# One visit of TensorE's column tiles for both value products of a full pair of key blocks, with the sums' PSUM bank lent to the scores

## The chip, the core and the metric

The program runs on one core of one Trainium2 chip. The metric is the device time of one execution in microseconds (us). TensorE multiplies matrices and writes PSUM, which has eight banks of 128 x 512 numbers of 32 bits; VectorE (DVE) and ScalarE (ACT) read PSUM; GpSimd (POOL) works in SBUF; SyncE (SP) and POOL issue DMAs. Semaphores are all that orders the engines against each other, and each engine runs its own list of instructions in order.

## The reference

Input x is 2 x 2048 x 512. A layer norm is followed by causal attention with 16 heads of 32 features (rotary positions on queries and keys), a residual, a second layer norm, and a linear layer with a routed low-rank part (8 experts, top 2) and a residual. The part that matters here:

```
scores = einsum('bhqd,bhkd->bhqk', q, k) / sqrt(32), later keys masked
attn = softmax(scores)              # needs each query's maximum and sum
ctx = einsum('bhqk,bhkd->bhqd', attn, v)
```

## The kernel before, in words

Three stages follow one another: `project` (queries, keys, values into scratch tensors in HBM), `attend`, and `finish`. The change touches `attend` alone.

**Groups, units, steps and pairs.** `attend` runs over 8 groups of 4 heads (`HG = 4`, `GROUPS = 8`). In a group the 2048 queries are 4 units of 512 (`QT`), and unit t meets its keys in blocks of 128: 4(t+1) steps, 40 in all (`STEPS`, `NSTEP`, L57). Two steps are a pair (`NPAIR = 20`). The last pairs of the units are 1, 5, 11 and 19 (`LAST_PAIR`). The last two pairs of each unit lie on the causal diagonal. The other 12 of a group are full: pairs 2, 3; 6 to 9; 12 to 17. `GATHER[p]` (L75) is set for exactly these, and says where their probabilities are added up for the sums.

**Scores.** Of each step four matmuls (`scores`, L970 to L983), one for each head, 98 x 128 by 98 x 512 in the full array, write 128 keys by 512 queries each into one of three PSUM banks of `a_st` in turn. ACT takes the exponential of each into the SBUF ring `a_probs` (L1077), which holds 4 steps; ACT fills a pair's places once the pair two before it has been used by the value product and added up (L1065 to L1071). A score waits until ACT is done with the bank (`wait_score_bank`, L786).

**Values.** `values` (L985 to L1000) multiplies a step's probabilities by the values of its 128 keys, for four heads at once: TensorE works there as four column tiles of 128 x 32 (`tile_position=(0, h * DK)`). The operands are of 32 bits, and each product is two matmul instructions in the trace, so that a step shows 8. All steps of a unit add up in one bank, `a_av`; ACT copies it out at the unit's end (L1062).

**Sums.** POOL adds the two steps of a pair (L936), in full pairs into the two buffers of `a_gather`, the later ones by way of `a_pair` and a DMA that accumulates (L833). `sums` (L1002 to L1026) multiplies by ones, also in column tiles, into the bank `a_sum`. It runs in the two diagonal pairs of a unit alone. At the start of the next unit's first pair (the opening pair: 2, 6, 12, or 0 of the next group) DVE transposes the bank (L1095, `turn_sums`, which raises `sum_turned`), inverts it (L1099) and turns it back (L1104). These three stand on DVE ahead of the first item of that pair, behind the first and behind the second.

**Items.** The softmax needs each query's maximum before its scores are taken. These maxima are found ahead of use by items: 140 in a group (`ITEMS`, `NITEM`), each one product of 96 x 128 by 96 x 512 (or less) in the full array into one of three banks of `a_mx` in turn (`item`, L957; `item_products`, L227), and one maximum on DVE (`item_max`, L241: a reduction at L249, or an addition of the mask and a maximum at L252). An item waits for the maximum of the one three before it (L967). A planner (`plan_items`, L107) spreads them over the pairs: 6 or 7 in most pairs, 8 in pairs 7 and 14, 6 in the opening pairs 2, 6 and 12. In the last group there are none from pair 10 on (`NO_ITEMS`); there the scores use six banks (three of `a_st`, three of `a_mx`), and DVE adds the pairs. In the first group the pairs 0 to 3 have 15 items each.

**TensorE's order** is written out in `group` (L1028 to L1043). Iteration p issues the scores of pair p+1 and the values of pair p, in two halves. A half takes half of the items, each followed by one of a step's four scores, and then one visit of the column tiles for one value product:

```python
for half, due in enumerate((items[:middle], items[middle:])):
    s = 2 * p + 2 + half
    for i in range(max(HG, len(due))):
        if i < len(due):
            item(...)
        if i < HG and s < NSTEP:
            scores(g, par, s, i)
    values(g, par, 2 * p + half)
sums(g, p)
```

PSUM is full: three banks of scores, three of items, one of values, one of sums.

Of the kernel before, what the change touches and what calls it, by code (L numbers as in the profile page):

```python
# [41 lines left out]
HG = 4  # L42
GROUPS = BATCH * HEADS // HG
QT = SEQ // TT
# [7 lines left out]
START = 1  # L52
# [4 lines left out]
STEPS = [(t, j) for t in range(QT) for j in range((t + 1) * SUB)]  # L57
NSTEP = len(STEPS)
# [4 lines left out]
LAST_PAIR = [e // 2 for e in UNIT_END]  # L63
# [11 lines left out]
GATHER = [gather_of(p) for p in range(NPAIR)]  # L75
# [46 lines left out]
def items_before(p, first):  # L122

    steady = PLAN[p % NPAIR] + NITEM * (p // NPAIR)
    return min(BEFORE_FIRST + PER_FIRST * p, steady) if first else steady
# [5 lines left out]


NO_ITEMS = min(p for p in range(NPAIR) if items_before(p, False) >= NITEM)


def units_ended_at_pair(p, first):
# [589 lines left out]
def attend(nc, block, qk_scr, v_scr, ctx_scr, shared, first, early):  # L726
    with ExitStack() as ctx:
# [6 lines left out]
        BANKS, MX_BANKS = 3, 3  # L734
# [14 lines left out]
        st_ps = ctx.enter_context(nc.psum_tensor("a_st", [P, BANKS, TT], F32))  # L749
        mx_ps = [ctx.enter_context(nc.psum_tensor(f"a_mx{n}", [P, TT], F32)) for n in range(MX_BANKS)]  # L750
        av_ps = ctx.enter_context(nc.psum_tensor("a_av", [P, TT], F32))
        sum_ps = ctx.enter_context(nc.psum_tensor("a_sum", [P, TT], F32))
# [8 lines left out]
        av_copied, sum_turned = early.av_copied, early.sum_turned  # L761
# [11 lines left out]
        def uses_before(n, of, banks):  # L773

            return n - banks if n >= banks else max(m for m in range(of) if m % banks == n) - of

        SIX_FROM = HG * (2 * NO_ITEMS + 2)

        def score_bank(g, n):

            if g < GROUPS - 1 or n < SIX_FROM:
                return st_ps[:, n % BANKS]
            m = (n - SIX_FROM) % (2 * BANKS)
            return st_ps[:, (SIX_FROM + m) % BANKS] if m < BANKS else mx_ps[m - BANKS][:, :]

        def wait_score_bank(pe, g, n):  # L786

            if g < GROUPS - 1 or n < SIX_FROM + BANKS:
                pe.wait_ge(exp_done, HG * NSTEP * g + uses_before(n, HG * NSTEP, BANKS) + 1 + BANKS)
            elif n < SIX_FROM + 2 * BANKS:  # L790
                pe.wait_ge(max_done, NITEM * GROUPS + MX_BANKS)
            else:
                pe.wait_ge(exp_done, HG * NSTEP * g + n - 2 * BANKS + 1 + BANKS)
# [162 lines left out]
        def _(pe):  # L956
# [13 lines left out]
            def scores(g, par, s, h):  # L970

                t, j = STEPS[s]
                q0 = max(0, j - t * SUB) * P
                if (g, h, t, j) == (0, 0, 0, 0):
                    pe.wait_ge(key_ones, 1)
                if (g, h, t, j) == (0, 0, 2, 2 * SUB):
                    pe.wait_ge(ones_copied, 4 * 16)
                if j == 0 and h == 0:
                    pe.wait_ge(shift_loaded[t % 2], SHIFTS * (2 * g + t // 2 + 1) + START)
                n = HG * s + h  # L980
                wait_score_bank(pe, g, n)
                block = keys[par][j // SUB][0:98, h, j % SUB * P:(j % SUB + 1) * P]
                pe.matmul(score_bank(g, n)[:, q0:TT], block, queries[t][0:98, h, q0:TT], start=True, stop=True).then_inc(st_done, 1)  # L983

            def values(g, par, s):  # L985

                t, j = STEPS[s]
                q0 = max(0, j - t * SUB) * P
                if j >= t * SUB:
                    pe.wait_ge(masked, diagonal_steps(g, s))  # L990
                else:
                    pe.wait_ge(exp_done, exps(g, s, HG - 1))
                if j == 0:
                    pe.wait_ge(av_copied, 4 * g + t + START)
                for h in range(HG):
                    mm = pe.matmul(av_ps[h * DK:(h + 1) * DK, q0:TT], vb[par][:, j, h * DK:(h + 1) * DK],  # L996
                                   probs[:, s % RING, h, q0:TT], start=j == 0, stop=s in UNIT_END,
                                   tile_position=(0, h * DK))
                if s % 2:
                    mm.then_inc(values_done, 1)  # L1000

            def sums(g, p):  # L1002

                s = 2 * p
                t, j = STEPS[s]
                if GATHER[p]:
                    return
                unit_first, unit_last = p == LAST_PAIR[t] - 1, p in LAST_PAIR
                q0, q1 = (max(0, j + n - t * SUB) * P for n in range(2))
                if unit_first:  # L1010
                    pe.wait_ge(sum_turned, 4 * g + t + START)
                if p in GATHERED_SUMS:
                    a = GATHERED_SUMS[p]
                    pe.wait_ge(gather_joined[a], 16 * joined(NPAIR * g + p, a))
                    for h in range(HG):
                        pe.matmul(sum_ps[h * DK:(h + 1) * DK, :], ones[:, :], gather[:, a, h, :], start=unit_first, stop=False,  # L1016
                                  tile_position=(0, h * DK))
                if q1 > q0:
                    for h in range(HG):
                        pe.matmul(sum_ps[h * DK:(h + 1) * DK, q0:q1], ones[:, :], probs[:, s % RING, h, q0:q1],  # L1020
                                  start=unit_first and p not in GATHERED_SUMS, stop=False, tile_position=(0, h * DK))
                pe.wait_ge(pair_added, 2 * (NPAIR * g + p) + 2)
                for h in range(HG):
                    mm = pe.matmul(sum_ps[h * DK:(h + 1) * DK, q1:TT], ones[:, :], pair[:, p % 2, h, q1:TT],  # L1024
                                   start=False, stop=unit_last, tile_position=(0, h * DK))
                mm.then_inc(pair_done, 1)  # L1026

            def group(g, par, use, next_use, first, last):  # L1028
                for p in range(NPAIR):
                    items = [(n, k) for n, k in items_of_pair(p, first) if not (n and last)]  # L1030
                    middle = (len(items) + 1) // 2
                    for half, due in enumerate((items[:middle], items[middle:])):
                        s = 2 * p + 2 + half
                        for i in range(max(HG, len(due))):
                            if i < len(due):
                                n, k = due[i]
                                item(g + n, (par + n) % 2, next_use if n else use, k)
                            if i < HG and s < NSTEP:
                                scores(g, par, s, i)
                            elif i < HG and not last:  # L1040
                                scores(g + 1, 1 - par, s - NSTEP, i)
                        values(g, par, 2 * p + half)
                    sums(g, p)  # L1043

            pe.wait_ge(first.mul_done, 4 * TILES + PROJECT_AHEAD)
# [662 lines left out]
```

## Time and profile before

| | |
|---|---|
| median of 3 runs | 1568.57 us (1568.54 to 1571.94) |
| the profiled execution | 1570.34 us |
| its span, first to last instruction | 1568.6 us |
| TensorE busy, mean granted clock | 98%, 0.998 |
| DVE, ACT, POOL busy | 73%, 49%, 57% |
| `attend` in the span | about 310 to 1296 us |
| one group of heads in the steady part | about 122.8 us (742.00 to 864.85, the same DVE instruction in two groups) |

A view of the chain of work follows what ended last back through what released it; its pieces show how long TensorE really spent on each group of matmuls. In the timeline a matmul's duration is modelled and overlaps the next one, so the distance from one start to the next is the figure to read. "PEld" is the loading of weights.

### The profile page before, as it was taken

How to read it: one execution, taken by the hardware profiler on the slowest of the kernel's cores; microseconds unless marked ns; L12 is line 12 of the kernel's file. 1: busy time of each engine (PE TensorE's matmuls, PEld its weight loads, DVE VectorE, ACT ScalarE, POOL GpSimd, SP SyncE). 2: the span in 40 equal slices, each digit the busy share in tenths (PEclk: the TensorE clock that was granted, in tenths of full speed). 3: DMA queues.
4: the chain of work that ended last, by engine and by line, in shares of the span. 5: the costliest groups of instructions: out<-in, count | busy, mean ns of one | idle time of the engine just before them, and what ended most of it. 6: DMA issues, size and time to landing. Idle time of an engine off the chain costs nothing.

```text
span 1568.6 us, 24836 instructions
## 1 busy us (share of the span) xinstructions
PE 1537.8 (98%) x9088; PEld 966.5 (62%) x9088; DVE 1141.6 (73%) x2269; ACT 767.6 (49%) x1540; POOL 890.7 (57%) x597
## 2 busy tenths in 40 slices
PE   6999999999999999999999999999999989999999
PEld 5888887755555555555555555555555537777777
DVE  6766666797777777777777777777777777656665
ACT  3222222236666656656666666665666673223221
POOL 2232322547778778787788797787787821121111
PEclk9999999999999999999999999999999999999999
DMA  5555685793485376377368359358444364222321
GB/s 201 208 198 191 214 270 193 201 195 70 86 173 127 85 166 143 82 150 167 83 135 189 82 123 201 81 107 197 96 92 122 85 145 132 81 81 86 143 67 54
DMA packets 120403, 215.83 MB, mean 138 GB/s; under 512 B 12504, under 2 KB 45784, under 8 KB 113112
## 3 DMA queue, kind: packets, MB, share of 16 engines
q1 hardware_dynamic: 102384, 136.20, 32.1%
q0 software_dynamic: 8064, 58.72, 18.2%
q10 hardware_dynamic: 9840, 19.40, 3.5%
q8 instruction: 69, 1.13, 0.3%
q14 instruction: 46, 0.38, 0.1%
HBM read 96.23 MB, written 58.72 MB: 99 GB/s over the span
## 4 chain that ended last, share of the span: by engine, by line
PE 90%; DVE 5%; DMA 2%; ACT 1%; issue 1%; SPq 0%; POOL 0%; DVEq 0%; POOLq 0%; ACTq 0%
PE a_mx L234 20%; PE a_av L996 16%; PE a_st L983 15%; PE p_pair L492 10%; PE f_wo_ps L1333 6%; PE f_out_ps L1393 5%; PE p_v L504 5%; PE a_sum L1016 2%; DVE a_part L249 2%; PE a_sum L1024 2%; PE f_out_ps L1408 1%; PE f_mid_ps L1333 1%; PE f_lg_ps L1363 1%; PE a_mx L238 1%; DMA a_gather<-a_pair 1%
## 5 line engine op out<-in xcount | busy, mean ns | idle before, releaser
L1077 ACT ACTIVATE a_probs<-a_st 128x512 f32<-128x512 f32 (+2 forms) x1244 | 584.6, 536 | 363.6 <-PE a_st L983 358.4
L249 DVE TENSOR_REDUCE a_part<-a_mx 128x1 f32<-128x512 f32 (+2 forms) x842 | 537.5, 680 | 104.3 <-PE a_mx L234 88.6
L936 POOL TENSOR_TENSOR a_pair<-a_probs 128x1024 f32<-128x1024 f32 (+2 forms) x224 | 397.8, 1800 | 39.4 <-ACT a_probs L1077 16.2
L936 POOL TENSOR_TENSOR a_gather<-a_probs 128x1024 f32<-128x1024 f32 x76 | 179.6, 2384 | 99.1 <-ACT a_probs L1077 99.1
L252 DVE CUSTOM_DVE_ANT_0 a_mx<-a_mx,f_ctx 128x384 f32<-128x384 f32 (+1 forms) x240 | 148.7, 632 | 86.8 <-PE a_mx L234 86.7
L366 POOL TENSOR_TENSOR p_rot<-p_mul 128x1024 f32<-128x1024 f32 x32 | 87.5, 2734 | 194.1 <-DVE p_mul L670 194.1
L1326 POOL TENSOR_TENSOR f_x<-f_x,f_bias 128x512 f32<-128x512 f32 x32 | 40.2, 1286 | 204.9 <-DVE f_xn L1543 204.9
L996 PE MATMUL a_av<-a_probs,a_v 128*32 128x512 f32 (+3 forms) x1280 | 149.8, 540 | 1.3 <-POOL a_probs L917 1.3
L996 PE MATMUL a_av<-a_probs,shared 128*32 128x512 f32 (+3 forms) x1280 | 150.9, 543 | 0.0
L917 POOL TENSOR_SCALAR_AFFINE_SELECT a_probs<-a_probs 128x512 f32<-128x512 f32 x128 | 89.8, 733 | 60.9 <-ACT a_probs L1077 60.7
L234 PE MATMUL a_mx<-a_k_stack,a_q_stack 96*128 96x512 f32 (+3 forms) x320 | 119.3, 397 | 0.0
L234 PEld LDWEIGHTS a_mx<-a_k_stack,a_q_stack 96*128 96x128 f32 x320 | 58.7, 189 | 71.6 <-DVE a_part L249 59.1
L983 PE MATMUL a_st<-a_q_stack,a_k_stack 98*128 98x512 f32 (+3 forms) x287 | 99.1, 366 | 1.4 <-DMA a_q_stack<-a_neg_rows 1.4
L578 ACT ACTIVATE p_rot_hi<-p_rot 128x1024 fp32r<-128x1024 f32 x32 | 34.0, 1061 | 110.1 <-POOL p_rot L366 94.3
L234 PE MATMUL a_mx<-a_k_stack,a_third 96*128 96x512 f32 (+3 forms) x192 | 73.6, 410 | 0.4
L674 DVE TENSOR_TENSOR p_rot_lo<-p_rot,p_rot_hi 128x1024 fp32r<-128x1024 f32 x28 | 45.8, 1635 | 36.6 <-ACT p_rot_hi L578 36.6
L492 PE MATMUL p_pair<-p_xt_lo,p_w_hi 128*128 128x512 f32 x256 | 69.9, 394 | 0.0
L833 POOL DMA_DIRECT2D a_gather<-a_pair x56 | 49.2, 879 | 33.9 <-POOL a_pair L936 15.1
L669 DVE TENSOR_TENSOR p_mul<-p_pair,p_tab 128x1024 f32<-128x1024 f32 x32 | 39.0, 1220 | 39.8 <-PE p_pair L492 39.8
L234 PE MATMUL a_mx<-a_k_stack,a_q_first 96*128 96x512 f32 (+3 forms) x192 | 65.3, 378 | 1.8 <-DVE a_part L249 1.1
L983 PE MATMUL a_st<-a_third,a_k_stack 98*128 98x512 f32 (+3 forms) x189 | 67.1, 375 | 0.0
L983 PEld LDWEIGHTS a_st<-a_q_stack,a_k_stack 98*128 98x128 f32 x287 | 53.9, 190 | 17.3 <-ACT a_probs L1077 8.2
(218 smaller groups left out, 2829.0 us busy)
## 6 DMA issues: line engine op xcount, KB each, us to landing
a_gather<-a_pair POOLq DMA_DIRECT2D x56, 1024.0 KB, 7.0
qk_scratch<-p_rot_hi SPq DMA_DIRECT2D x32, 512.0 KB, 3.1
qk_scratch<-p_rot_lo SPq DMA_DIRECT2D x32, 512.0 KB, 3.9
a_k_stack<-qk_scratch SPq DMA_DIRECT2D x60, 256.0 KB, 8.1
a_q_first<-qk_scratch SPq DMA_DIRECT2D x48, 256.0 KB, 6.6
a_third<-qk_scratch SPq DMA_DIRECT2D x36, 256.0 KB, 5.5
v_scratch<-p_v_st SPq DMA_DIRECT2D x32, 256.0 KB, 7.1
ctx_scratch<-a_ctx_st SPq DMA_DIRECT2D x32, 256.0 KB, 2.8
```

Of the source, the lines that this page charges most:

```text
L234: mm = pe.matmul(places[:, i, :], queries[0:96, head, qi * P:(qi + 1) * P], keys[0:96, head, 0:width], start=(i == 0), stop=not masked_her ...
L249: dve.tensor_reduce(found, scores.rearrange("p (h n) -> p h n", n=width), AX.X, ALU.max).then_inc(self.max_done, 1)
L252: dve.tensor_tensor_reduce(out=scores, in0=scores, in1=self.mask[:, TT - width:TT], scale=1.0, scalar=3.0 * MASKED, op0=ALU.add, op1=ALU.m ...
L366: pool.tensor_tensor(rot[:, par], mul[:, par, :, 0, :], mul[:, par, :, 1, :], ALU.add).then_inc(rot_done, 1)
L492: mm = pe.matmul(pair_ps[p % 2][:, half, :], w[:, kt, cols], a[u][:, kt, :], start=(n == 0), stop=(n == len(passes) - 1))
L504: mm = pe.matmul(v_ps[s % 2][:, :], a[u][:, kt, s * P:(s + 1) * P], w[:, kt, 2 * DM:3 * DM], start=(n == 0), stop=(n == len(passes) - 1))
L917: pool.affine_select(block, block, pattern=[[0, HG], [1, P]], compare_op=ALU.is_ge, fill=0.0, base=0, channel_multiplier=-1).then_inc(mask ...
L936: pool.tensor_tensor(place[:, h:h + 2, q0:TT], probs[:, s % RING, h:h + 2, q0:TT], probs[:, (s + 1) % RING, h:h + 2, q0:TT], ALU.add).then ...
L983: pe.matmul(score_bank(g, n)[:, q0:TT], block, queries[t][0:98, h, q0:TT], start=True, stop=True).then_inc(st_done, 1)
L996: mm = pe.matmul(av_ps[h * DK:(h + 1) * DK, q0:TT], vb[par][:, j, h * DK:(h + 1) * DK], probs[:, s % RING, h, q0:TT], start=j == 0, stop=s ...
L1077: act.activation(probs[:, s % RING, h, q0:TT], score_bank(g, HG * s + h)[:, q0:TT], ACT.Exp, scale=SCORE_SCALE).then_inc(exp_done, 1)
L1333: mm = pe.matmul(out, w, a, start=(n == 0), stop=(n == len(pairs) - 1))
```

## The change

In iterations with a full pair (`GATHER[p]`) the two halves become one: all items of the pair, interleaved with all eight scores of the two steps ahead, then both value products in one visit of the column tiles. In the other iterations the two halves stay.

The eight scores in a row get a fourth bank: the bank of the sums, which is idle while full pairs are worked on. A plan (`plan_banks`) gives each score of the two-half and one-visit iterations its bank, the one used longest ago, with the fourth allowed in full iterations only and, in an opening iteration, from the third score on. The first score in it there waits for the transposition of the sums (`sum_turned`); the first sums of a unit wait for the exponential of the last score that lay in their bank.

```diff
+def plan_banks():
+    banks, behind, ahead_of_sums, last_use = {}, {}, {}, [None] * SCORE_BANKS
+    for n in range(-2 * HG, GROUPS * SCORES - 2 * HG):
+        g, p, i = n // SCORES, n % SCORES // (2 * HG), n % (2 * HG)
+        score = n + 2 * HG
+        if score >= SCORES * (GROUPS - 1) + SIX_FROM:
+            break
+        opens = n >= 0 and p - 1 in LAST_PAIR
+        if n >= 0 and GATHER[p] and opens and i == 0:
+            last_use = last_use[:SCORE_BANKS] + [-(QT * g + STEPS[2 * p][0])]
+        usable = range(SCORE_BANKS + 1 if n >= 0 and GATHER[p] and not (opens and i < 2) else SCORE_BANKS)
+        bank = min(usable, key=lambda b: -1 if last_use[b] is None else max(0, last_use[b]))
+        banks[score], behind[score], last_use[bank] = bank, last_use[bank], score
+        if bank == SUM_BANK:
+            ahead_of_sums[QT * g + STEPS[2 * p][0]] = score
...
         def score_bank(g, n):
             if g < GROUPS - 1 or n < SIX_FROM:
-                return st_ps[:, n % BANKS]
+                bank = BANK_OF_SCORE[SCORES * g + n]
+                return sum_ps[:, :] if bank == SUM_BANK else st_ps[:, bank]
...
         def wait_score_bank(pe, g, n):
-            if g < GROUPS - 1 or n < SIX_FROM + BANKS:
-                pe.wait_ge(exp_done, HG * NSTEP * g + uses_before(n, HG * NSTEP, BANKS) + 1 + BANKS)
+            if g < GROUPS - 1 or n < SIX_FROM:
+                behind = BANK_BEHIND[SCORES * g + n]
+                if behind is not None and behind < 0:
+                    pe.wait_ge(sum_turned, -behind + START)
+                elif behind is not None:
+                    pe.wait_ge(exp_done, behind + 1 + BANKS)
...
                 if unit_first:
                     pe.wait_ge(sum_turned, 4 * g + t + START)
+                    if QT * g + t in AHEAD_OF_SUMS:
+                        pe.wait_ge(exp_done, AHEAD_OF_SUMS[QT * g + t] + 1 + BANKS)
...
                     middle = (len(items) + 1) // 2
-                    for half, due in enumerate((items[:middle], items[middle:])):
-                        s = 2 * p + 2 + half
-                        for i in range(max(HG, len(due))):
+                    visits = [(items, (0, 1))] if GATHER[p] else [(items[:middle], (0,)), (items[middle:], (1,))]
+                    for due, steps in visits:
+                        ahead = [(2 * p + 2 + half, h) for half in steps for h in range(HG)]
+                        for i in range(max(len(ahead), len(due))):
...
-                        values(g, par, 2 * p + half)
+                        for half in steps:
+                            values(g, par, 2 * p + half)
```

The banks of the items stay three, and their order and number in each pair stay as they are. No engine's instructions change in number or shape.

## Rows read from the trace of the kernel before

**Rows 1.** The page: busy time of the engines, and the chain's shares by engine.

```profile
PE 1537.8 (98%) x9088; PEld 966.5 (62%) x9088; DVE 1141.6 (73%) x2269; ACT 767.6 (49%) x1540; POOL 890.7 (57%) x597
...
PE 90%; DVE 5%; DMA 2%; ACT 1%; issue 1%; SPq 0%; POOL 0%; DVEq 0%; POOLq 0%; ACTq 0%
```

**Rows 2.** One stretch of steady attention: busy us and instructions of PE, PEld, DVE, ACT, POOL.

```profile
820.00:940.00 120.00, 119.45 (x809) 64.34 (x812) 93.32 (x201) 75.92 (x162) 96.94 (x66) 1.00 0.59 129
```

**Rows 3.** The chain, 700 to 760 us: start, us, engine, tile, line.

```profile
710.80 0.36 PE a_av L996 x8
...
734.38 0.86 PE a_sum L1016 x8
...
737.59 0.99 PE a_av L996 x8
```

**Rows 4.** Timeline of full pairs 7 and 8, 736 to 757 us: start, us, engine.

```profile
742.16 2.06 ACT L1077 ACTIVATE a_probs<-a_st 128x512 f32<-128x512 f32 x4 [0.81 <-PE a_st L983]
...
743.05 0.39 PE L983 MATMUL a_st<-a_third,a_k_stack 98*128 98x512 f32 x1
743.38 1.06 PE L996 MATMUL a_av<-a_probs,a_v 128*32 128x512 f32 x8
744.37 0.44 PE L234 MATMUL a_mx<-a_k_stack,a_q_stack 96*128 96x384 f32 x1
...
747.38 0.50 PE L234 MATMUL a_mx<-a_k_stack,a_q_stack 96*128 96x512 f32 x1
747.72 0.40 PE L983 MATMUL a_st<-a_third,a_k_stack 98*128 98x512 f32 x1
747.96 0.40 PE L234 MATMUL a_mx<-a_k_stack,a_q_stack 96*128 96x512 f32 x1
```

**Rows 5.** Timeline, 400 to 445 us: first item of a half, and DVE's maxima.

```profile
436.76 0.50 PE L234 MATMUL a_mx<-a_k_stack,a_third 96*128 96x512 f32 x1
...
437.30 2.48 DVE L249 TENSOR_REDUCE a_part<-a_mx 128x1 f32<-128x512 f32 x4 [1.08 <-PE a_mx L234]
```

**Rows 6.** Timeline of opening pair 6, a steady group: TensorE's first item, then DVE.

```profile
735.61 0.50 PE L234 MATMUL a_mx<-a_k_stack,a_q_stack 96*128 96x512 f32 x1
...
735.75 0.72 DVE L1095 STREAM_TRANSPOSE a_sum_t<-a_sum 128x512 f32<-128x512 f32 x1 [1.34 <-PE a_sum L1024]
...
736.39 0.65 DVE L249 TENSOR_REDUCE a_part<-a_mx 128x1 f32<-128x512 f32 x1
...
738.28 0.53 DVE L252 CUSTOM_DVE_ANT_0 a_mx<-a_mx,f_ctx 128x384 f32<-128x384 f32 x1
```

**Rows 7.** Opening pair 2 of the first group, eight items in its first half: timeline.

```profile
332.74 0.45 PE L234 MATMUL a_mx<-a_third 96*128 96x384 f32 x1
...
335.46 0.65 DVE L249 TENSOR_REDUCE a_part<-a_mx 128x1 f32<-128x512 f32 x1
...
336.17 0.50 PE L234 MATMUL a_mx<-a_k_first,a_third 96*128 96x512 f32 x1 [0.69 <-DVE a_part L249]
```

**Rows 8.** Pair 1 of the first group, second half, eight items: timeline.

```profile
323.88 0.50 PE L234 MATMUL a_mx<-a_k_first,a_third 96*128 96x512 f32 x1
...
324.42 3.68 DVE L249 TENSOR_REDUCE a_part<-a_mx 128x1 f32<-128x512 f32 x6 [0.88 <-PE a_mx L234]
...
327.55 0.51 PE L234 MATMUL a_mx<-a_k_first,a_third 96*128 96x512 f32 x1 [0.16 <-DVE a_part L249]
```

**Rows 9.** Waits, 400 to 1250 us: waiter, releaser, us in total, times, longest.

```profile
ACT a_probs L1077 <- PE a_st L983: 312.0, 325, 3.0
...
DVE a_sum_t L1095 <- PE a_sum L1024: 17.5, 20, 1.3
...
PE a_mx L234 <- DVE a_part L249: 1.9, 7, 0.3
```

**Rows 10.** The last group without items, timeline: first visits of two iterations in a row.

```profile
1262.07 1.07 PE L996 MATMUL a_av<-a_probs,a_v 128*32 128x512 f32 x8
...
1266.31 1.06 PE L996 MATMUL a_av<-a_probs,a_v 128*32 128x512 f32 x8
```

More of the change, by code:

```diff
@@ L133 @@
 NO_ITEMS = min(p for p in range(NPAIR) if items_before(p, False) >= NITEM)
+SCORES = HG * NSTEP
+SIX_FROM = HG * (2 * NO_ITEMS + 2)
+SCORE_BANKS = 3
+SUM_BANK = SCORE_BANKS
+def plan_banks():
[13 more added lines that the diff above has]
+            ahead_of_sums[QT * g + STEPS[2 * p][0]] = score
+    return banks, behind, ahead_of_sums, sorted(range(SCORE_BANKS), key=lambda b: last_use[b]), last_use
+BANK_OF_SCORE, BANK_BEHIND, AHEAD_OF_SUMS, OLDEST_FIRST, LAST_USE = plan_banks()
 def units_ended_at_pair(p, first):
@@ L775, in uses_before @@
             return n - banks if n >= banks else max(m for m in range(of) if m % banks == n) - of
-        SIX_FROM = HG * (2 * NO_ITEMS + 2)
         def score_bank(g, n):
             if g < GROUPS - 1 or n < SIX_FROM:
-                return st_ps[:, n % BANKS]
+                bank = BANK_OF_SCORE[SCORES * g + n]
+                return sum_ps[:, :] if bank == SUM_BANK else st_ps[:, bank]
             m = (n - SIX_FROM) % (2 * BANKS)
-            return st_ps[:, (SIX_FROM + m) % BANKS] if m < BANKS else mx_ps[m - BANKS][:, :]
+            return st_ps[:, OLDEST_FIRST[m]] if m < BANKS else mx_ps[m - BANKS][:, :]
         def wait_score_bank(pe, g, n):
-            if g < GROUPS - 1 or n < SIX_FROM + BANKS:
-                pe.wait_ge(exp_done, HG * NSTEP * g + uses_before(n, HG * NSTEP, BANKS) + 1 + BANKS)
+            if g < GROUPS - 1 or n < SIX_FROM:
[4 more added lines that the diff above has]
+                    pe.wait_ge(exp_done, behind + 1 + BANKS)
+            elif n < SIX_FROM + BANKS:
+                pe.wait_ge(exp_done, LAST_USE[OLDEST_FIRST[n - SIX_FROM]] + 1 + BANKS)
             elif n < SIX_FROM + 2 * BANKS:
@@ L1037, in group @@
                                 item(g + n, (par + n) % 2, next_use if n else use, k)
[L1038 to L1041, printed above, removed]
-                        values(g, par, 2 * p + half)
+                            if i < len(ahead):
+                                s, h = ahead[i]
+                                if s < NSTEP:
+                                    scores(g, par, s, h)
+                                elif not last:
+                                    scores(g + 1, 1 - par, s - NSTEP, h)
+                        for half in steps:
+                            values(g, par, 2 * p + half)
                     sums(g, p)
```

## The prediction

> **What bounds the kernel now.** I read the page first. TensorE is busy for 98% of the span and is 90% of the chain that ended last; DVE is 5% [rows 1]. A busy matmul row only says that one was in flight, so the next view is the stretch of steady attention: in 120 us TensorE is busy 119.45 us, DVE 93.32, ACT 75.92, POOL 96.94 [rows 2]. The waits say the same from the other side: ACT waits for TensorE's scores 312 us in 850, DVE waits for the sums 20 times (some 28 units end in that stretch), and TensorE itself is held by DVE for 1.9 us [rows 9]. So TensorE's own time sets the pace, and DVE has some 22% to spare on average. Whether it has it at the right moment is the question of this case.
>
> The last view, the timeline of full pairs, shows what a visit of the column tiles costs beyond its work. Read starts, not durations. Full-array matmuls follow each other every 0.235 us (0.24 from the first score to the next item) [rows 4]. (a) From the last score to the visit it is 0.33 us: 0.10 too much. (b) The visit takes 0.99 us for 512 queries and 0.36 for 128, hence 0.21 per 128 queries and 0.84 to 0.86 for the work itself; a product that follows inside the same visit takes 0.86 [rows 3], so 0.13 is entry. (c) The first item after it takes 0.34 us to the next start [rows 4], 0.10 too much, since its weights were not loaded ahead. Together 0.33 us a visit.
>
> **What the change takes away.** One visit in each full pair: 12 pairs in 8 groups, 96 visits. 96 x 0.33 = 31.7 us, all on TensorE and so on the path, if nothing takes its place. The Trainium skill ("TensorEngine Tiling (Array Packing)", Key Properties) says that changing the tiling mode drains the engine, which is the same gap told as a mechanism; by that rule alone the time would fall by those 31.7 us.
>
> **What it adds: items in one burst.** Number and order of the items stay, but all of a pair now stand ahead of one long visit of 0.99 + 0.86 = 1.85 us, where each half with its 3 or 4 items had a visit behind it in which DVE caught up. An item waits for the maximum of the one three before. The prices: DVE starts 0.54 us after the first item starts (436.76 to 437.30), takes 0.60 us an item (four take 2.48, six take 3.68, the last ends 0.68 after its start) [rows 5, 8], and a waiting item starts 0.06 us after the maximum it waits for (335.46 + 0.65, then 336.17) [rows 7]. Its successor is then 0.10 us later too, as in (c). Items in a burst would start at 0, 0.575, and every 0.47 from there, since a score stands between.
>
> *Regular full pairs* (3; 7 to 9; 13 to 17). Item k is needed at 0.575 + 0.47(k-1) and can start at 0.54 + 0.60(k-3) + 0.68 + 0.06. For the sixth item (k = 5) that is 2.45 against 2.48; for the seventh 2.92 against 3.08, with the 0.10 a delay of 0.26; for the eighth 3.39 against 3.68, a delay of 0.39. The present kernel has such a burst, eight items in a half of the first group's pair 1: the eighth starts at 327.55, 0.06 behind its maximum (324.42 + 4 x 0.60 + 0.68 = 327.50) [rows 8]. So a pair of seven gains 0.33 - 0.26 = 0.07 us and a pair of eight loses 0.06. A group has seven of the first and two of the second: 0.37 us gained, 2.7 us over the groups (the last has four such pairs with items).
>
> The same page's Performance Considerations ("PSUM Bottleneck") speak against the change: tiling speeds up TensorE but not the emptying of PSUM, which may become the bottleneck. The trace agrees for a burst (0.60 us an item against 0.47) and not for the average [rows 2]. By that rule alone regular pairs would gain nothing and the sum would be 2.7 us higher.
>
> *Opening pairs* (2, 6, 12). DVE transposes the sums ahead of the first maximum and turns the inverse back behind the second. In pair 6 TensorE's first item starts at 735.61, and DVE reaches the first maximum at 736.39 and the third at 738.28, 2.67 us behind [rows 6]. Now half a pair, three items, ends there and no item waits. In the burst the sixth item needs the third maximum: 2.67 + 0.65 + 0.06 = 3.38 us, where it could have started at 2.45. The wait is 0.93, with the successor's 0.10 it is 1.03 us; less 0.33 the pair is 0.70 us slower. The first group's pair 2 shows the very wait: the sixth item of its half of eight starts 3.43 us after the first, and the wait named is for DVE [rows 7]. Three in each of seven groups and two in the last (12 has no items there): 23 x 0.70 = 16.1 us. No later wait gives this back, as TensorE has almost none [rows 9].
>
> **The other edits.** *The fourth bank of scores:* ACT needs 2.06/4 = 0.515 us a score [rows 4] against TensorE's 0.47; with three banks the last of eight would wait some 0.1 to 0.2 us, with four none: nought here. *The wait for `sum_turned`* in front of the third score: that score is due 0.34 + 0.94 = 1.28 us behind the first item, the transposition ends 0.14 + 0.72 = 0.86 behind it [rows 6], with a release of 0.06 and 0.10 for weights 1.02: covered by 0.26 us. If DVE were later by one maximum (0.60), 0.35 us would show. Queued behind this wait are all items and values of the pair. *The wait of the first sums* for an exponential two iterations old: covered by a whole iteration, nought. *Values one visit later:* `values_done` rises at an iteration's end as now, and ACT, which fills the ring behind it, idles waiting for TensorE [rows 9]; POOL's additions (96.94 of 120) move up to 1.2 us within the iteration and have a whole one until ACT asks; no DMA is moved past another. Nought.
>
> **The tail of the last group.** Pairs 12 to 17 have no items. An iteration takes 4.24 us (1262.07 to 1266.31) [rows 10]. New, TensorE needs 8 x 0.235 + 0.33 + 1.71 = 3.9 us and ACT 8 x 0.515 = 4.12 [rows 4]: ACT bounds, 0.12 x 6 = 0.7 us gained; nothing, if the joining DMAs bound there, and 2.0 at most.
>
> **Sum.** -2.7 + 16.1 - 0.7 = +12.7 us. The profiled execution took 1570.34 us (span 1568.6, 1.7 around it), 1.8 above the median of 1568.57; counted from the median: 1581 us. What a measurement of this kernel can tell from no change is about 0.3%, 4.7 us.
>
> **Bounds.** The opening pairs' net can lie between -0.33 (no wait) and +1.1 (DVE late by another 0.4); I take 0.70 for the two rows that show it. The regular pairs' lies between -0.17 (each maximum 0.1 us less late, since masked items of 384 columns are shorter) and +0.1. That makes 1562 to 1594 without a change of mechanism.
>
> **Rivals.**
> 1. *DVE keeps up: faster.* Its 22% of idle time [rows 2] speaks for it; the bursts of rows 7 and 8 speak against. It decides at the items' wait: if the seventh item of a regular pair and the sixth of an opening one start without one, 90 pairs gain 0.33 and the tail 0.7: 1538 us. 12%. Where only the openings' wait is a third of what I say (0.3 us), it is 23 x 0 - 6 (the regular pairs at -0.09) - 0.7: 1562 us, 6%.
> 2. *No difference that can be told.* The opening pairs cost 0.2 to 0.3 us each, as DVE's transposition moves ahead or the long visit hides part: 23 x 0.25 - 3.4 = +2.4: 1571 us. 14%.
> 3. *The lent bank costs as well.* DVE is not idle when the sums end in some 8 cases of 28 [rows 9], and the third score waits 0.35 us in every opening: +8 us, 1589; if it also pushes the items, up to 1600. 12%.
> 4. *The change does not save the visit.* The second product pays its own 0.33: +43 us, 1611. The 0.86 behind a value product [rows 3] excludes it nearly: 2%.
>
> My own forecast, 1581, has 54%. Left out of a range of 1557 to 1595 are rival 1's full form, rival 4 and the end of rival 3, some 17%. Faster 0.18, same 0.14, slower 0.68.
>
> **What the profile of the changed kernel would show.** Two value products as one piece of about 1.85 us, and no first-item gap between them. In opening pairs the sixth item about 3.4 us behind the first, its wait put down to DVE; in regular pairs the seventh at about 3.1. TensorE's waits for DVE in 400 to 1250 us up from 1.9 to 20 us or more, DVE idle mostly during the long visits. A group of heads at about 124.5 us (122.8 + 3 x 0.70 - 0.37). I am wrong if the group is at or below 122.8, or if the waits at the items are there and the group is not longer: then TensorE had slack that I did not see.

## The result, and the profile after

The changed kernel takes 1581.09 us (median of 9 runs) against 1570.0 us for the kernel before on the same chip: ratio 1.0071, 95% interval 1.005 to 1.0093, or 8 to 15 us slower. The forecast was 1581 us, 12.7 us above the median of before. One of the nine executions of the kernel before took 5023.35 us; the median hardly depends on it. Executions of one kernel spread by some 11 us with the mean granted clock (the kernel before in another series: 1567.48 us at 1.000, 1579.02 us at 0.991), so that two medians that lie less than about 3 us apart are not told apart here.

The page of the changed kernel, its busy times and the chain's shares by engine, beside [rows 1]:

```profile
PE 1539.3 (97%) x9088; PEld 966.1 (61%) x9088; DVE 1133.5 (72%) x2269; ACT 767.4 (49%) x1540; POOL 890.3 (56%) x597
...
PE 86%; DVE 10%; DMA 1%; issue 1%; ACT 1%; SPq 0%; POOL 0%; DVEq 0%; POOLq 0%; ACTq 0%
```

The instructions are the same in number. DVE did no more work than before, yet its share of the chain went from 5% to 10%: TensorE now stands behind it. The same stretch of steady attention as [rows 2] (busy us of PE, PEld, DVE, ACT, POOL):

```profile
820.00:940.00 120.00, 117.88 (x801) 63.35 (x799) 90.44 (x197) 75.43 (x160) 93.23 (x64) 1.00 0.56 125
```

TensorE has lost 1.6 us of its 119.45, and every other engine did less in the 120 us: the whole pipeline runs slower. The waits of TensorE for DVE in 400 to 1250 us (in total, times, longest): first the line of the kernel before that [rows 9] leaves out, beside its 1.9 us behind L249, then the two of the changed kernel:

```profile
PE a_mx L234 <- DVE a_part L252: 1.0, 6, 0.2
...
PE a_mx L262 <- DVE a_part L277: 9.1, 20, 0.6
PE a_mx L262 <- DVE a_part L280: 3.7, 13, 0.4
```

Together 2.9 us before and 12.8 us now. These lines understate the waits, since a matmul's modelled duration covers part of one: the sixth item below is given 0.38 us of waiting, but it starts 0.78 us behind the score before it (742.64), where 0.235 is usual. So the distances between starts are read here. Opening pair 6 of a steady group, which answers to [rows 6], in the timeline:

```profile
740.11 0.50 PE L262 MATMUL a_mx<-a_k_stack,a_q_stack 96*128 96x512 f32 x1
...
740.25 0.72 DVE L1134 STREAM_TRANSPOSE a_sum_t<-a_sum 128x512 f32<-128x512 f32 x1 [1.34 <-PE a_sum L1059]
...
740.88 0.65 DVE L277 TENSOR_REDUCE a_part<-a_mx 128x1 f32<-128x512 f32 x1
...
742.16 0.69 DVE L1143 STREAM_TRANSPOSE a_rsum_b<-a_rsum 128x512 f32<-128x512 f32 x1
...
742.78 0.53 DVE L280 CUSTOM_DVE_ANT_0 a_mx<-a_mx,f_ctx 128x384 f32<-128x384 f32 x1
...
743.42 0.50 PE L262 MATMUL a_mx<-a_k_stack,a_q_stack 96*128 96x512 f32 x1 [0.38 <-DVE a_part L280]
...
744.56 1.93 PE L1029 MATMUL a_av<-a_probs,a_v 128*32 128x512 f32 x16
...
746.42 0.44 PE L262 MATMUL a_mx<-a_k_stack,a_q_stack 96*128 96x384 f32 x1
```

DVE reaches the third maximum (742.78) 2.67 us behind the pair's first item, to the hundredth as before, and the sixth item (743.42) stands right behind it, 3.31 us after the first. The visit is one piece of 16 instructions. The iteration takes 6.31 us (740.11 to 746.42); before it took 5.76, from 735.61 [rows 6] to 741.37. Three more lines of that iteration of the kernel before: its last two scores of the first half, the visit, and the next pair's first item:

```profile
736.82 0.76 PE L983 MATMUL a_st<-a_third,a_k_stack 98*128 98x512 f32 x2
...
737.52 1.06 PE L996 MATMUL a_av<-a_probs,a_v 128*32 128x512 f32 x8
...
741.37 0.44 PE L234 MATMUL a_mx<-a_k_stack,a_q_stack 96*128 96x384 f32 x1
```

From the first of the two scores to the visit it is 0.70 us, where 0.235 + 0.33 would do: the kernel before already lost 0.13 us in this pair, to a score that waited until ACT was done with its bank. In the changed kernel the chain runs over DVE at the sixth item (start, us, engine, tile, line):

```profile
742.16 0.69 DVE a_rsum_b L1143
742.85 0.46 DVE a_mx L280
743.42 0.50 PE a_mx L262
...
744.63 1.85 PE a_av L1029 x16
```

Opening pair 2 of the next group suffers more. Its two ends in the timeline:

```profile
839.73 0.50 PE L262 MATMUL a_mx<-a_third,a_q_stack 96*128 96x512 f32 x1
...
846.44 0.50 PE L262 MATMUL a_mx<-a_third,a_q_stack 96*128 96x512 f32 x1
```

6.71 us against 5.78: DVE first has the five short operations that end a unit's maxima, and reaches the transposition of the sums 0.52 us behind the first item (840.25), in pair 6 only 0.14. Pair 12 takes 6.37 against 5.90. The three openings of a group together are 1.95 us longer, 0.65 each.

A regular pair of eight items, pair 7 (its first item, its eighth, its visit, the next pair's first item):

```profile
746.42 0.44 PE L262 MATMUL a_mx<-a_k_stack,a_q_stack 96*128 96x384 f32 x1
...
750.05 0.45 PE L262 MATMUL a_mx<-a_k_stack,a_q_stack 96*128 96x512 f32 x1
...
750.65 1.92 PE L1029 MATMUL a_av<-a_probs,a_v 128*32 128x512 f32 x16
...
752.51 0.50 PE L262 MATMUL a_mx<-a_k_stack,a_q_stack 96*128 96x512 f32 x1
```

The eighth item comes 3.63 us behind the first, the pair takes 6.09 us against 6.01 [rows 4]: what the spared visit gave went to the waits. A whole group, from one masked maximum of pair 7 to the same one a group later (747.05 to 871.45), takes 124.40 us against 122.85: 1.55 more. Less the 1.95 of the openings, the nine regular pairs are 0.40 us faster together. For the changed kernel that is the longest of six groups: over the second to the seventh group the mean is 124.11 us against 122.73, or 1.38 more. By the medians of these six, the regular pairs are far from equal: 3, 13, 15, 16 and 17 gain 0.10 to 0.22 us, pair 8 gains 0.02, 7 and 14 lose 0.06 and 0.10, and pair 9 loses 0.23. In pair 9 the seventh item, the first of the next group, stands behind scores of 384 columns, and its wait for DVE grew from 0.29 to 0.61 us (before, after):

```profile
757.82 0.64 PE L234 MATMUL a_mx<-a_k_first,a_q_first 96*128 96x128 f32 x4 [0.29 <-DVE a_part L249]
...
762.30 0.64 PE L262 MATMUL a_mx<-a_k_first,a_q_first 96*128 96x128 f32 x4 [0.61 <-DVE a_part L277]
```

The tail of the last group, first visits of two iterations in a row, beside [rows 10]:

```profile
1272.71 1.92 PE L1029 MATMUL a_av<-a_probs,a_v 128*32 128x512 f32 x16
1276.76 1.92 PE L1029 MATMUL a_av<-a_probs,a_v 128*32 128x512 f32 x16
```

4.05 us where it was 4.24; over the five distances from 1272.71 to the sixth visit at 1293.14 the mean is 4.09. Nothing of it reaches the end of the stage. From the start of pair 12's iteration in the last group to the last transposition of the sums it is 35.46 us before and 36.62 us after. In pair 18 the first value product waits for POOL, which masks the probabilities of the diagonal; the wait was 1.29 us in the kernel before:

```profile
1297.99 1.94 PE L1029 MATMUL a_av<-a_probs,a_v 128*32 128x512 f32 x8 [2.26 <-POOL a_probs L950]
```

### The profile page after: what moved, and what is told of

Its sections match the earlier page's. It is cut to its first block, busy times and chain, and to the rows that moved or that the text cites. A ratio compares the mean times of both kernels' runs of the same rounds, so it can differ in the third digit from the quotient of the medians.

```text
span 1579.4 us, 24843 instructions
## 1 busy us (share of the span) xinstructions
PE 1539.3 (97%) x9088; PEld 966.1 (61%) x9088; DVE 1133.5 (72%) x2269; ACT 767.4 (49%) x1540; POOL 890.3 (56%) x597
## 4 chain that ended last, share of the span: by engine, by line
PE 86%; DVE 10%; DMA 1%; issue 1%; ACT 1%; SPq 0%; POOL 0%; DVEq 0%; POOLq 0%; ACTq 0%
PE a_mx L262 18%; PE a_av L1029 16%; PE a_st L1016 11%; PE p_pair L520 10%; PE f_wo_ps L1372 6%; PE f_out_ps L1432 5%; PE p_v L532 5%; DVE a_part L277 5%; PE a_sum L1016 2%; PE a_sum L1051 2%; PE a_sum L1059 2%; PE f_out_ps L1447 1%; PE f_mid_ps L1372 1%; PE f_lg_ps L1402 1%; DVE a_rsum_b L1143 1%
## 5 line engine op out<-in xcount | busy, mean ns | idle before, releaser
L1116 ACT ACTIVATE a_probs<-a_st 128x512 f32<-128x512 f32 (+1 forms) x1064 | 512.5, 531 | 363.8 <-PE a_st L1016 337.5
L1029 PE MATMUL a_av<-a_probs,a_v 128*32 128x512 f32 (+3 forms) x1280 | 141.4, 542 | 2.3 <-POOL a_probs L950 2.3
L1029 PE MATMUL a_av<-a_probs,shared 128*32 128x512 f32 (+3 forms) x1280 | 141.8, 543 | 0.0
L262 PE MATMUL a_mx<-a_k_stack,a_q_stack 96*128 96x512 f32 (+3 forms) x320 | 123.4, 409 | 3.8 <-DVE a_part L277 1.8
L1116 ACT ACTIVATE a_probs<-a_sum 128x512 f32<-128x512 f32 (+1 forms) x180 | 105.7, 587 | 10.8 <-PE a_sum L1016 8.6
L1016 PE MATMUL a_st<-a_q_stack,a_k_stack 98*128 98x512 f32 (+3 forms) x243 | 84.8, 360 | 0.8 <-DMA a_q_stack<-a_neg_rows 0.8
L1029 PEld LDWEIGHTS a_av<-a_probs,a_v 128*32 128x32 f32 x1280 | 30.4, 109 | 61.0 <-issue 39.1
```

The source lines that it names most:

```text
L262: mm = pe.matmul(places[:, i, :], queries[0:96, head, qi * P:(qi + 1) * P], keys[0:96, head, 0:width], start=(i == 0), stop=not masked_her ...
L1116: act.activation(probs[:, s % RING, h, q0:TT], score_bank(g, HG * s + h)[:, q0:TT], ACT.Exp, scale=SCORE_SCALE).then_inc(exp_done, 1)
```

## The experiments

Theory: the items of a full pair, 6 to 8 in one burst, wait for their three banks, that is for DVE, above all in the opening pairs, where DVE's two transpositions stand among the maxima. Rivals: each merged visit costs a little; the lent bank and its wait for the transposition cost. Ratios are against the kernel before on the same chip. What the traces say of the opening pairs and of a whole group stands in a table behind the experiments.

**Openings put back into two halves.**

```diff
-visits = [(items, (0, 1))] if GATHER[p] else [...]
+visits = [(items, (0, 1))] if GATHER[p] and not p - 1 in LAST_PAIR else [...]
```

> The changed kernel with the opening pairs (2, 6, 12) put back into two halves; the nine other full pairs keep one visit. My theory (the loss sits in the opening pairs, where DVE's two transpositions stand ahead of the maxima that the burst of items needs): the 11 us are gone, the time is 0 to 4 us below the kernel before, about 1568 us, and a group of heads takes 122.5 us. Rival (each merged visit costs a little, since DVE falls behind in every burst): three quarters of the merged pairs are left, so 8 us of the 11 stay, about 1578 us. Rival (the lent bank costs): the bank is still lent in the openings, so 1581 us stays.

1570.34 us, ratio 0.9986 (0.9966 to 1.0006): level with the kernel before (1570.14 us in this series), where 0 to 4 us below it were expected; a group takes 122.25 us in the trace, where 122.5 were. The loss is gone with three of twelve merged pairs, while nine stay merged. The rival that each merged visit costs a little falls.

**The opposite: one visit in the openings alone.**

```diff
-visits = [(items, (0, 1))] if GATHER[p] else [...]
+visits = [(items, (0, 1))] if GATHER[p] and p - 1 in LAST_PAIR else [...]
```

> The opposite of e1: one visit in the opening pairs alone, two halves in the nine other full pairs. My theory: all of the loss stays, 1580 to 1585 us. Rival (every burst costs a little): a quarter of the 11 us, about 1573 us.

1583.33 us, ratio 1.007 (1.0044 to 1.0096): the whole loss, from a quarter of the merged pairs.

**DVE turns the inverse back last.**

```diff
-                        for unit in ended:
-                            if i == 0:
-                                invert(*unit)
-                            if i == 1:
-                                turn_back(*unit)
...
+                    for unit in ended:
+                        invert(*unit)
+                        turn_back(*unit)
```

> The changed kernel with DVE's inversion and its turning back of the sums moved behind all items of the opening pair; the first transposition stays where it is. My theory: the third maximum of an opening pair then ends at about 0.78 + 1.2 + 0.65 = 2.6 us instead of 3.3 us behind the first item, the sixth item waits 0.1 to 0.2 us instead of 0.9, and the kernel returns to within 3 us of the one before: 1568 to 1573 us. Rival (the third score waits for the transposition of the sums in the lent bank): that transposition has not moved, so 1581 us stays. Rival (POOL's division waits for the turned inverse and holds its additions): slower than 1581 us.

1567.75 us, ratio 0.9971 (0.9954 to 0.9988), some 13 us below the changed kernel and just under the range expected. The rival of POOL's division, which wanted a slower kernel, falls too. The same opening pair in its timeline (first item, first two maxima, third maximum, sixth item, next pair's first item):

```profile
730.99 0.50 PE L262 MATMUL a_mx<-a_k_stack,a_q_stack 96*128 96x512 f32 x1
...
731.76 1.25 DVE L277 TENSOR_REDUCE a_part<-a_mx 128x1 f32<-128x512 f32 x2
...
732.94 0.56 DVE L280 CUSTOM_DVE_ANT_0 a_mx<-a_mx,f_ctx 128x384 f32<-128x384 f32 x1
...
733.63 0.46 PE L262 MATMUL a_mx<-a_k_stack,a_q_stack 96*128 96x512 f32 x1
...
736.58 0.45 PE L262 MATMUL a_mx<-a_k_stack,a_q_stack 96*128 96x384 f32 x1
```

The third maximum starts 1.95 us behind the first item instead of 2.67, the sixth item 2.64 instead of 3.31, and the iteration takes 5.59 us instead of 6.31. The transposition of the sums, for which the lent bank waits, did not move (0.13 us behind the first item, 0.14 in the changed kernel), so the lent bank is not the cause. The move took 0.70 us off each of the three openings. It did more than undo the loss: a group takes 122.03 us against 122.73 in the kernel before, so with the burst's wait shortened the merged visits begin to pay.

**The same order in the kernel before**, as a control (the edit is the one above, the rest is the kernel before):

> The kernel before (two halves everywhere) with DVE's inversion and turning back moved behind the opening pair's items, as in e2. It tells whether e2's gain of 13 us against the changed kernel is the removal of the burst's wait or a gain that this order gives anyway. My theory: in two halves no item waits for the turning back, so nothing moves: 1570 us, within 2 us. Rival (the order gains by itself): 1557 to 1562 us.

1570.23 us, ratio 0.9998 (0.998 to 1.0016). The order gains nothing where items come in halves; in e2 it took away a wait that the burst had made.

**Three banks for the scores.**

```diff
-usable = range(SCORE_BANKS + 1 if n >= 0 and GATHER[p] and not (opens and i < 2) else SCORE_BANKS)
+usable = range(SCORE_BANKS)
```

> The changed kernel with one visit, but the scores keep three banks and the sums' bank is never lent. My theory: ACT's 0.515 us a score against TensorE's 0.47 us costs 0.1 us at the end of a burst at most, and often nothing where an item waits anyway: 0 to 6 us above the changed kernel, 1581 to 1587 us. Rival (the lent bank's wait for the transposition is what costs): 8 us below the changed kernel, about 1573 us.

1583.17 us, ratio 1.0066 (1.0039 to 1.0092). Without the lent bank the change costs the same, and the opening pairs take the same time to 0.01 us (6.70, 6.29 and 6.37): the bank neither hurts nor helps where the items wait anyway.

**The lent bank alone, two halves everywhere.**

```diff
-visits = [(items, (0, 1))] if GATHER[p] else [(items[:middle], (0,)), (items[middle:], (1,))]
+visits = [(items[:middle], (0,)), (items[middle:], (1,))]
```

> The changed kernel with two halves and two visits everywhere, and the lent fourth bank for the scores alone. My theory: the scores hardly wait for a bank, so 0 to 2 us below the kernel before, 1569 us. Rival (the lent bank's wait for the transposition costs): 1575 us or more.

1569.34 us, ratio 0.9993 (0.9973 to 1.0014): nothing that can be told. In the trace pair 6 takes 5.60 us instead of 5.76: the score that waited for its bank in the kernel before waits no longer.

**One visit, and the bank goes to the items.** Starting from the kernel before, with the merged visits of the change:

```diff
+def plan_item_banks():
...
+                usable = range(MAX_BANKS + 1 if GATHER[p] and not (opens and i < 3) else MAX_BANKS)
+                bank = min(usable, key=lambda b: -1 if last_use[b] is None else max(0, last_use[b]))
...
-                pe.wait_ge(max_done, NITEM * g + uses_before(k, NITEM, MX_BANKS) + 1 + MX_BANKS)
-                first.item_products(pe, mx_ps[k % MX_BANKS], k, queries[t], keys[par][c])
+                behind = ITEM_BEHIND[NITEM * g + k]
+                if behind is not None and behind < 0:
+                    pe.wait_ge(sum_turned, -behind + START)
+                elif behind is not None:
+                    pe.wait_ge(max_done, behind + 1 + MX_BANKS)
+                first.item_products(pe, item_bank(g, k), k, queries[t], keys[par][c])
```

> The merged visit of the change, but the sums' bank is lent to the items as a fourth bank in full pairs (from the fourth item on in an opening pair) and the scores keep three banks. My theory (items, not scores, lack a bank): an item then waits for the maximum of the one four before, 0.60 us later slack, so the seventh and eighth items of a regular pair no longer wait, and the sixth of an opening pair waits for the second maximum instead of the third; the 0.33 us of each merged visit stays as gain in most pairs: 17 to 22 us below the kernel before, about 1551 us. Rival (DVE as a whole cannot keep the pace, whatever the banks): 1575 us or more.

1548.34 us, ratio 0.9852 (0.983 to 0.9874), 22.4 us below the kernel before of its series (17 to 22 were expected). So the spared visits are worth having once the items have a bank more: same DVE, same order on it, same number of maxima. "DVE as a whole cannot keep the pace" falls. The profiled execution took 1558.18 us, 10 us above the median; the lines are from a stretch at a granted clock of 1.00. Its opening pair (first item, the fourth item in the bank `a_sum`, the sixth, the last three scores, the visit, the next first item):

```profile
735.33 0.50 PE L260 MATMUL a_mx<-a_k_stack,a_q_stack 96*128 96x512 f32 x1
...
736.77 0.40 PE L260 MATMUL a_sum<-a_k_stack,a_q_stack 96*128 96x512 f32 x1
...
737.71 0.39 PE L260 MATMUL a_mx<-a_k_stack,a_q_stack 96*128 96x512 f32 x1
737.94 1.32 PE L1018 MATMUL a_st<-a_third,a_k_stack 98*128 98x512 f32 x3
739.19 1.92 PE L1031 MATMUL a_av<-a_probs,a_v 128*32 128x512 f32 x16
741.05 0.45 PE L260 MATMUL a_mx<-a_k_stack,a_q_stack 96*128 96x384 f32 x1
```

The sixth item comes 2.38 us behind the first, without a wait. But the last three scores take 1.25 us to the visit, where three unhindered ones take 0.8: with items out of the way the scores wait for their banks (the weight loads of the last two are held 0.30 us each until ACT is done).

**The bank for the items, two visits** (the same plan of banks in the kernel before, halves kept):

> The kernel before with the fourth bank for the items alone; two halves and two visits stay. My theory: few items wait in halves, so about 5 us are gained (mostly in pair 9, whose seventh item now waits for the one two before): 1565 us. The distance from e6, 12 to 16 us, is then what the merged visits give once items do not wait. Rival (the bank is what gains, the visit gives nothing): the same time as e6.

1564.99 us, ratio 0.9965 (0.9953 to 0.9977): 5.5 us from the bank. The 16.6 us between this and e6 (12 to 16 were expected) are the merged visits.

**Both: e6 with the turning back last** (the two edits above together):

> e6 with e2's order on DVE. My theory: with four banks the sixth item of an opening pair needs only the second maximum, so the order of the turning back gives little more: 0 to 4 us below e6, about 1550 us. If the openings still wait in e6 it is more than that.

1545.64 us, ratio 0.9851 (0.983 to 0.9873). Medians 2.7 us apart, intervals the same: little more, as expected.

**The price of a visit.** e6, with the eighth score between the two value products:

```diff
+                        kept = ahead.pop() if len(steps) == 2 else None
...
                         for half in steps:
+                            if half == 1 and len(steps) == 2:
+                                issue_score(kept)
                             values(g, par, 2 * p + half)
```

> e6 with the last of the eight scores moved between the two value products, so that the column tiles are visited twice again while the burst of items stays as it is. It prices a visit by itself. My theory (0.33 us a visit: 0.13 entry, 0.10 before, 0.10 after): 96 x 0.33 = 32 us at most above e6; items that still wait a little get some of it back, so 24 to 32 us above e6, 1572 to 1580 us. Rival (most of e6's gain is the order and the bank, a visit costs little): within 10 us of e6, 1558 us or less.

1566.01 us, ratio 0.9972 (0.9958 to 0.9986), 17.7 us above e6: between theory and rival, and outside both ranges. It ran beside another series of the kernel before than e6, but the two medians of that kernel differ by only 0.12 us. The timeline shows the price itself (product, score, product, first item):

```profile
739.52 1.07 PE L1031 MATMUL a_av<-a_probs,a_v 128*32 128x512 f32 x8
740.51 0.50 PE L1018 MATMUL a_st<-a_third,a_k_stack 98*128 98x512 f32 x1
740.95 1.06 PE L1031 MATMUL a_av<-a_probs,a_v 128*32 128x512 f32 x8
741.94 0.44 PE L260 MATMUL a_mx<-a_k_stack,a_q_stack 96*128 96x384 f32 x1
```

From 739.52 to 741.94 it is 2.42 us; in e6 the one visit takes 1.86 (739.19 to 741.05) and a score 0.235: 2.10. The difference, 0.32 us, is the price forecast. What is missing from 96 x 0.33 = 32 us lies in single pairs: by the medians of the six steady groups e10 is 0.30 to 0.34 us longer than e6 in pairs 7, 9, 14 and 16, which is the whole price, but only 0.07 to 0.12 us in the openings and in pair 13 (pair 6: 5.80 against 5.72). The reading is that there the scores' wait in e6 is hidden by the score moved away. The six visits of the tail bring nothing to the end of the stage either.

**Scores first.** To test that reading: e8, with each score of a burst ahead of its item.

```diff
-                            if i < len(due):
+                            if i < len(due) and len(steps) == 1:
                                 n, k = due[i]
                                 item(g + n, (par + n) % 2, next_use if n else use, k)
...
+                            if i < len(due) and len(steps) == 2:
+                                n, k = due[i]
+                                item(g + n, (par + n) % 2, next_use if n else use, k)
```

> e8 with each score of a merged burst ahead of its item instead of behind it. It tests why e10 lay only 18 us above e6 where 96 visits at 0.33 us are 32 us. My theory: in e6 and e8 the last scores of a burst wait for one of their three banks (0.45 us in an opening pair, some 0.2 in pairs of seven items), 14 us in all, which e10 hid; scores issued 0.24 us earlier find their banks free earlier, while the items, with four banks, can afford 0.24 us: 4 to 14 us below e8, about 1538 us. Rival (the 14 us lie elsewhere, as in the rows of maxima that arrive late by DMA): e8's time or above, 1545 to 1552 us, since the items and so the maxima come later.

1539.46 us, ratio 0.9793 (0.9767 to 0.9818): 6.2 us below e8 (7.7 us when each is counted from the kernel before of its own series), and the fastest of all. So about half of the 14 us was the scores' waits, as thought; where the other half lies, no run shows. Its opening pair (first score, last item, last two scores, visit, next pair):

```profile
723.11 0.50 PE L1018 MATMUL a_st<-a_third,a_k_stack 98*128 98x512 f32 x1
...
725.73 0.40 PE L260 MATMUL a_mx<-a_k_stack,a_q_stack 96*128 96x512 f32 x1
725.96 0.85 PE L1018 MATMUL a_st<-a_third,a_k_stack 98*128 98x512 f32 x2
726.74 1.92 PE L1031 MATMUL a_av<-a_probs,a_v 128*32 128x512 f32 x16
728.59 0.50 PE L1018 MATMUL a_st<-a_third,a_k_stack 98*128 98x512 f32 x1
```

5.48 us an opening, against 5.72 in e6, 5.76 before and 6.31 in the changed kernel. In the steady stretch DVE now works 96.22 us of 120, more than in any other kernel here, and TensorE is busy all the time:

```profile
820.00:940.00 120.00, 119.74 (x834) 68.72 (x836) 96.22 (x209) 77.46 (x169) 99.78 (x69) 1.00 0.63 136
```

**The openings and a group in all traces.** Times in us from an iteration's first item (in e11 its first score) to the next iteration's; medians over the second to the seventh group, the last column the mean of those six.

| kernel | pair 2 | pair 6 | pair 12 | a group |
|---|---|---|---|---|
| before | 5.76 | 5.76 | 5.91 | 122.73 |
| changed | 6.70 | 6.30 | 6.37 | 124.11 |
| e1, openings in halves | 5.74 | 5.60 | 5.91 | 122.25 |
| e4, openings alone in one visit | 6.70 | 6.29 | 6.37 | 124.36 |
| e2, turned back last | 6.00 | 5.60 | 5.67 | 122.03 |
| e3, three banks for the scores | 6.70 | 6.29 | 6.37 | 124.13 |
| e8, the bank to the items, turned back last | 5.73 | 5.72 | 5.83 | 119.41 |
| e11, scores first | 5.48 | 5.48 | 5.59 | 118.18 |

## Why the prediction was right

- **The visit's price, 0.33 us**, held: 0.32 measured in e10, and two products in one visit take 1.85 us as said. In the changed kernel the openings and pairs 7, 9 and 14 spent more than it on waits, and the other regular pairs kept 0.02 to 0.22 us of it.
- **Opening pairs.** Forecast: sixth item 3.38 us behind the first, 0.70 us slower each. Measured in pair 6: 3.31 and 0.55; over the three openings 0.93, 0.55 and 0.47, mean 0.65. The mechanism is shown by e1, e4, e2 and e5. The size was off by pair. In pair 6 the sixth item came 0.07 us sooner than priced, since the third maximum is of 384 columns, and the kernel before had already lost 0.13 us there to a score's wait, where the forecast took its halves to be free of waits. In pair 12 the sixth item came 3.38 us behind the first, exactly as priced (903.88 to 907.26); why the pair still lost only 0.47 was not taken apart. In pair 2 the end of a unit's maxima comes on top, which I had left out.
- **Regular pairs.** Forecast 0.37 us gained in nine; measured 0.40 in one group, some 0.3 by the medians of six. The sum agrees partly by luck: every pair of seven items was to gain 0.07, but five gained 0.10 to 0.22 and pair 9 lost 0.23. The burst was priced with scores of 512 columns and items of one kind. Pair 7 lost 0.08 where 0.06 was forecast.
- **The group**: forecast 124.5 us, measured 124.40 in the longest and 124.11 in the mean; 1.38 us more than before in the mean, where 1.7 was forecast.
- **The tail**: 4.12 us an iteration forecast, 4.09 measured, but the 0.7 us that the sum took off for it did not reach the end of the stage (35.46 us from pair 12 before; 36.62 in the changed kernel; 35.62, 35.68 and 35.66 in e2, e6 and e11). The forecast had named this case ("nothing, if the joining DMAs bound there") without choosing it. In the trace of the changed kernel TensorE waits there for POOL's masks.
- **The other edits at nothing**: right for the lent bank (e3, e9). In opening pair 2 the first score in the lent bank starts on time (0.24 us behind the item before it, 840.78 to 841.02); the item behind it is late (841.56) because it needs the bank of the first maximum, which DVE ends at 841.50.
- **A sign that failed**: TensorE's waits for DVE were to rise from 1.9 to 20 us or more in 400 to 1250 us; the view says 12.8. The group is longer all the same. The forecast priced waits by starts, and this view leaves a part of each out.
- **The sum**, 12.7 us against 11.1 between the medians, is well inside the interval. That the time itself, 1581 us, was met to 0.1 us is luck: the median of the kernel before was 1570.0 us beside the changed kernel, and the forecast counted from 1568.57.
- **The bounds**, "1562 to 1594", do not follow from the nets they name: added straight, 23 openings from -0.33 to +1.1 us and 67 regular pairs from -0.17 to +0.1 us give 1549 to 1600 us. The range stated at the end, 1557 to 1595, is narrower than that too.
- **Rival 1**, the average idle time of DVE, failed as the bursts of [rows 7, 8] said. Its 22% were real, as e6 and e11 show, but were reached to a small part by DVE's order (e2) and for the rest with a bank more. By the Trainium skill ("TensorEngine Tiling (Array Packing)", Performance Considerations) the emptying of PSUM may become the bottleneck after tiling. The page speaks of the products of tiles, and the banks that DVE empties here hold full-array products; with that difference the trace agrees for bursts with three banks (TensorE waits 12.8 us for DVE in 400 to 1250 us), and not with four (1.0 us in e6 and in e8).
- **Where an expectation failed**: e10's. I multiplied a true price by 96 without asking what else the moved score would change. Four more lie less than 1 us outside their ranges: e1, e2, e6, and the distance from e7 to e6.

## What to carry to other kernels

An engine that is idle for a fifth of the time can still set the pace, if the work is handed to it in bursts longer than its buffers: compare the n-th hand-over with the end of the one n minus buffers before, burst by burst, before merging anything. When a merged stage needs one more buffer, ask which of the two streams in it has the slower consumer (here 0.60 us against 0.47 us of supply for the items, 0.515 for the scores) and give the buffer to that one. The bank lent to the scores changed nothing (e3, e9); lent to the items it turned 11 us lost into 22 us gained. Then look at the consumer's own order: what nobody waits for soon (the turned inverse) goes behind what the producer needs next.

## What the runs showed of the hardware that was not expected

A product in column tiles that follows another in the same visit costs nothing beyond its columns (1.85 us for two against 0.99 for one), so the price lies in the change between full-array and column-tile work in either direction: 0.32 to 0.33 us there and back.

One maximum stands out without a cause that I could find: in pair 13 of the fourth group DVE starts the first one 0.98 us behind its item (785.85 and 786.83 us in the changed kernel), where the same kind in pair 7 starts after 0.63 us (746.42 and 747.05). It is the same in the kernel before (780.02 and 781.00), and only in that group: a group later pair 13 starts its own after 0.62 us (910.26 and 910.88) and takes 5.62 us instead of 5.97. This stays open.
